# Attention's two z evacuations move from ScalarE to VectorE, and the FFN's last two output groups are emitted as a closure one iteration later

## What is computed

```python
def attn(x):                       # x is layernorm(x)
    q, k, v = x @ Wq.T, x @ Wk.T, x @ Wv.T          # 16 heads x 128
    s = clip(q @ k.T / sqrt(128), -1024, 1024)
    s = s + slope[h] * j + causal(i, j)             # ALiBi bias, causal mask
    return softmax(s) @ v  ->  @ Wo
def ffn(x):                        # x is layernorm(x)
    base = x @ W.T + b
    gates = softmax(top2(x @ gate_w.T + gate_b))    # 8 experts, rank 16
    return base + sum_over_top2(gate * (x @ A_e.T @ B_e.T))
x = x + attn(layernorm(x)); x = x + ffn(layernorm(x))
```

## Time and profile before

| what | us |
|---|---|
| median of the two runs shown | 4926.32 (4838.13 and 5014.51) |
| the profiled execution | 4846.59 |
| its span on the slowest core, 7 | 4845.0 |
| the spans of the eight cores | 4811.6 to 4845.0 |

### The profile page before, as it was taken

One profiled execution on the slowest core, in us unless ns is written; L12 is line 12 of the kernel. 1 busy time (PEld: TensorE's weight loads), 2 busy tenths in 40 slices (PEclk: granted clock), 3 DMA queues, 4 the chain that ended last, 5 costly groups with the idle time before them and its releaser, 6 DMA issues. The chain is left out here.

```text
span 4845.0 us, 65585 instructions; the slowest of 8 cores (4811.6 to 4845.0 us)
## 1 busy us (share of the span) xinstructions
PE 3632.1 (75%) x18452; PEld 1694.7 (35%) x18452; DVE 1615.0 (33%) x4336; ACT 1491.2 (31%) x3694; POOL 110.7 (2%) x210
## 2 busy tenths in 40 slices
PE   3578788898987794676734687888888878937677
PEld 1233344443433341233312343434444433413333
DVE  2222434535353111222312334344453531112223
ACT  5442442525343100212144525334252431001211
POOL 0000000000000001000000000000000000010000
PEclk7668778898988896777867687788889888967778
DMA  3201101011111655111132011110101126451111
GB/s 112 57 14 22 18 14 27 14 23 18 22 20 35 166 157 105 61 61 61 53 109 66 14 23 18 18 23 14 27 14 23 18 45 172 148 105 61 61 61 53
DMA packets 55538, 258.39 MB, mean 53 GB/s; under 512 B 13720, under 2 KB 13984, under 8 KB 34720
## 3 DMA queue, kind: packets, MB, share of 16 engines
q0 software_dynamic: 36464, 119.66, 12.3%
q1 hardware_dynamic: 11824, 84.20, 5.4%
q10 hardware_dynamic: 6912, 50.33, 2.9%
HBM read 273.15 MB, written 67.11 MB: 70 GB/s over the span
## 5 line engine op out<-in xcount | busy, mean ns | idle before, releaser
L812 DVE TENSOR_SCALAR sp<-ps 128x512 f32<-128x512 f32 (+3 forms) x1104 | 634.7, 596 | 227.8 <-ACT prT L876 119.8
L851 ACT ACTIVATE prT<-dg,cstt 128x128 bf16<-128x128 f32 (+1 forms) x576 | 217.6, 388 | 1580.5 <-DVE dg L823 1252.4
L1119 PE MATMUL cb<-wf,cT 128*128 128x512 bf16 x2048 | 536.6, 426 | 83.5 <-DMA wf<-wf 81.8
L876 ACT ACTIVATE prT<-sp,cstt 128x128 bf16<-128x128 f32 (+2 forms) x1368 | 582.3, 494 | 4.6 <-DVE zc L752 1.0
L805 PE MATMUL ps<-QT,KT 128*128 128x512 bf16 (+3 forms) x1104 | 457.2, 481 | 111.5 <-DVE sp L812 67.4
L420 PE MATMUL bp<-wo,zTt 128*128 128x512 bf16 x2048 | 468.1, 392 | 89.7 <-DMA wo<-wo 71.5
L632 PE MATMUL pp<-xnT,wv 128*128 128x512 bf16 x2048 | 485.1, 400 | 0.4
L632 PE MATMUL pp<-xnT,wq 128*128 128x512 bf16 x2048 | 462.0, 387 | 0.0
L632 PE MATMUL pp<-xnT,wk 128*128 128x512 bf16 x2048 | 457.6, 384 | 0.0
L743 PE MATMUL pz<-va,prT 128*128 128x129 bf16 x3652 | 376.3, 258 | 20.7 <-ACT prT L876 9.3
L1119 PEld LDWEIGHTS cb<-wf,cT 128*128 128x128 bf16 x2048 | 216.1, 108 | 389.2 <-issue 210.2
(11 more groups left out here) (105 smaller groups left out, 2463.4 us busy)
## 6 DMA issues: line engine op xcount, KB each, us to landing
bx<-x SPq DMA_DIRECT2D x32, 1024.0 KB, 6.7
x2d<-b POOLq DMA_DIRECT2D x32, 1024.0 KB, 8.8
c<-x2d ACTq DMA_DIRECT2D x32, 1024.0 KB, 4.8
out<-co SPq DMA_DIRECT2D x32, 1024.0 KB, 3.9
prT<-x ACTq DMA_DIRECT2D x16, 1024.0 KB, 4.9
prT<-x SPq DMA_DIRECT2D x16, 1024.0 KB, 5.0
wv<-wv POOLq DMA_DIRECT2D x32, 512.0 KB, 5.3
wq<-wq POOLq DMA_DIRECT2D x32, 512.0 KB, 5.2
```

The source lines that it names most:

```text
L812: lambda e, n=n, bank=bank, buf=buf: e.tensor_scalar(spanb[buf][:, 0:n], psc[bank][:, 0:n], 1024.0, -1024.0, ALU.min, ALU.max),
L851: soff=soff: e.activation(probsT[:, pslot:pslot + min(ncols, 128)], diagb[:, soff:soff + min(ncols, 128)] if ncols == 64 else diagb[:, 0:128],
L876: buf=buf, bcol=bcol: e.activation(probsT[:, pslot: pslot + ncols], spanb[buf][:, soff: soff + ncols], AF.Exp, bias=cst[:, bcol:bcol + 1]),
L1119: lambda e, bi=bi, dc=dc, og=og, bk=bk: e.matmul(b["pb"][bk][:, :], b["xnT2"][bi][:, dc * 128:(dc + 1) * 128], b["wfT"][:, dc * D + og * 5 ...
```

## The change

Two things. In attention, the multiplication of `pz` by the reciprocal and the copy of the transposed block are DVE instructions in place of ACT ones, with the waits changed to match. In the FFN, `finish_og(2)`, `finish_og(3)` and the store become a closure that is called at the top of the next iteration.

```diff
-        first_w.append((s_act, st["pz_guard"][qt % 2]))
+        first_w.append((s_dve, st["pz_guard"][qt % 2]))
...
-        zn = pg.op("scalar",
-                   lambda e, zb=zb, qt=qt: e.activation(
-                       ztm[zb][:, :], pz[qt % 2][:, 0:128], AF.Identity,
-                       scale=zcol[:, 4 + qt % 2:5 + qt % 2]),
-                   inc=s_act,
+        zn = pg.op("vector",
+                   lambda e, zb=zb, qt=qt: e.tensor_scalar(
+                       ztm[zb][:, :], pz[qt % 2][:, 0:128],
+                       zcol[:, 4 + qt % 2:5 + qt % 2], None, ALU.mult),
+                   inc=s_dve,
                    waits=[(s_dve, r), (s_pe, st["ztr_tok_pe"][zb])])
...
-                       waits=[(s_act, zn), st["ptp_copy"]])
+                       waits=[(s_dve, zn), st["ptp_copy"]])
             st["ztr_tok_pe"][zb] = zt
-            st["ptp_copy"] = (s_act, pg.op(
-                "scalar",
-                lambda e, h=h, qt=qt: e.activation(
+            st["ptp_copy"] = (s_dve, pg.op(
+                "vector",
+                lambda e, h=h, qt=qt: e.tensor_copy(
                     zT[:, h * SEQL + qt * 128: h * SEQL + (qt + 1) * 128],
-                    ptp[:, 0:128], AF.Identity),
-                inc=s_act, waits=[(s_pe, zt)]))
+                    ptp[:, 0:128]),
+                inc=s_dve, waits=[(s_pe, zt)]))
...
+    pend_fin = []
     for i in range(NT):
         bi = i % 2
         bi3 = i % 3
+        for _f in pend_fin:
+            _f()
+        pend_fin.clear()
         t_apply = apply_tok[bi3]
...
         base_chunks(2)
         base_chunks(3)
-        finish_og(2, False)
-        mm = finish_og(3, False)
...
+        def fin23(fi=i, fbi=bi, fbi3=bi3, fev4=ev4, ffinish=finish_og):
+            nonlocal wxa_reader
+            ffinish(2, False)
+            mm = ffinish(3, False)
...
+        pend_fin.append(fin23)
+    for _f in pend_fin:
+        _f()
+    pend_fin.clear()
```

More of the change, by code:

```diff
@@ L1155, in _plan_ffn, with finish_og @@
                                (s_pe, wxa_reader)])
-        def finish_og(og, first_delta):
+        def finish_og(og, first_delta, fi=i, fbi=bi, fbi3=bi3, fev4=ev4,
+                      fwxa_tok=wxa_tok):
             bk = og % 2
@@ L1164, in finish_og @@
                       inc=s_pe,
-                      waits=[lora_tok[4]] if (i == 0 and og == 0) else [])
+                      waits=[lora_tok[4]] if (fi == 0 and og == 0) else [])
             m = pg.op("tensor",
@@ L1171, in finish_og @@
                       inc=s_pe,
-                      waits=([(s_dve, wxa_tok)] if first_delta else []) +
-                            ([lora_tok[3]] if (i == 0 and og == 0) else []))
+                      waits=([(s_dve, fwxa_tok)] if first_delta else []) +
+                            ([lora_tok[3]] if (fi == 0 and og == 0) else []))
             ev = pg.op("vector",
-                       lambda e, bi=bi, bi3=bi3, og=og, bk=bk: e.tensor_tensor(
-                           b["outb"][bi][:, og * 512:(og + 1) * 512],
+                       lambda e, fbi=fbi, fbi3=fbi3, og=og, bk=bk:
+                       e.tensor_tensor(
+                           b["outb"][fbi][:, og * 512:(og + 1) * 512],
                            b["pb"][bk][:, :],
-                           b["x2b"][bi3][:, og * 512:(og + 1) * 512], ALU.add),
+                           b["x2b"][fbi3][:, og * 512:(og + 1) * 512],
+                           ALU.add),
                        inc=s_dve,
-                       waits=[(s_pe, m), (sem["dob"][bi], store_tok[bi])])
+                       waits=[(s_pe, m), (sem["dob"][fbi], store_tok[fbi])])
             base_evac[bk] = ev
-            ev4[og] = ev
+            fev4[og] = ev
             return m
@@ L1188, in _plan_ffn @@
         base_chunks(3)
-        finish_og(2, False)
-        mm = finish_og(3, False)
[L1191 to L1198, removed]
+        def fin23(fi=i, fbi=bi, fbi3=bi3, fev4=ev4, ffinish=finish_og):
+            nonlocal wxa_reader
+            ffinish(2, False)
+            mm = ffinish(3, False)
+            wxa_reader = mm
+            xnT2_rd[fbi] = mm
+            ev_out[fbi3] = fev4[-1]
+            store_tok[fbi] = pg.op("sync",
+                                   lambda e, fi=fi, fbi=fbi: e.dma_start(
+                                       out_d.ap()[seq][fi],
+                                       b["outb"][fbi][:, :]),
+                                   inc=sem["dob"][fbi], amt=16,
+                                   waits=[(s_dve, t_) for t_ in fev4])
+        pend_fin.append(fin23)
+    for _f in pend_fin:
+        _f()
+    pend_fin.clear()
 def _host_consts():
```

## The result

The changed kernel takes 1.004 times as long as before, with an interval of 1.0025 to 1.0055: some 19 us slower. Ratios compare fast runs with fast runs; in a slow one the cores of one die show a lower granted clock and take longer. The prediction took 2% as what a measurement of this kernel can tell from no change; the interval is much narrower than that. The forecast had +56 us, with a sum of single terms behind it of +104 and -48. The direction of each term was right, and the small net is what two large terms leave. Both were off, by amounts that add.

The account below looks back on a forecast made before the run. ACT was taken to bound heads 0 to 5, ACT and DVE together the group heads. Over two sequences 104 - 48 = +56 us on 4846.6 gives 4903, stated as 4900; range 4835 to 4965.

Parts of the forecast that it names:

- What bounds the kernel: Attention stretches: ACT is fullest in heads 0 to 5; in group heads ACT (31.91 us) and DVE (29.04) are almost level.
- The price of a block: Per query block, DVE gains 0.19 wait, 0.27 multiplication and 0.14 copy, 0.60 us in all; ACT loses 0.41 us.
- The stretch after: Attention stretches set by DVE's time: heads 0 to 5 give back 24.0 us per sequence, ten group heads cost 52.
- The 9.6: DVE's added time per attention stretch, from 0.60 us for each query block.
- The 2.0: Time per stretch DVE can't fill: 0.6 us before the first clip and the end of the last two accumulations.
- DVE is the fullest engine in every head: All attention stretches: with ACT down by 6.6 us and DVE up by 9.6, DVE is the fullest engine.
- The second way of the prediction: Group heads: ten early blocks cost 6.0 us, six find idle time in the tail; between +5 and +6 us.
- FFN: FFN half of the change: every engine's order and waits stay the same, cost 0.
- The signs: What would show it: DVE busy up 230 us, ACT down 210, group stretches 43 us with DVE at 90% or more.
- A: Group stretches: DVE has room, so not slower; 4799 us, or 4636 if every stretch gains 6.6 us; chance 0.15.
- B: Group stretch tails: PE's clock stays at 1.2 GHz, total 5000 us, 3.2% slower; chance 0.14.
- C: FFN: the change hides the tail of a tile behind the next, below 20 us; chance 0.01.

Follow-up runs that it names:

- the early blocks: Against the kernel before, both instructions on DVE only in the first nine query blocks (qt 0 to 8) of the group heads: profiled execution 4915.9 us.
- the hidden wait: Against the attention half alone, transpose and copy of the block before emitted between reciprocal and multiplication: profiled execution 4799.8 us, group stretches 40.24 us.
- the second copy: Against the attention half alone, DVE copies the transposed block a second time, into a scratch tile, in every block: ratio 1.0104 (1.0026 to 1.0182).
- the late blocks: Against the kernel before, both instructions on DVE only in the last seven query blocks (qt 9 to 15) of the group heads: ratio 0.9978.

## Why the prediction was right or wrong

**What bounds the kernel.** Right. The page's shares of 33% and 31% said nothing; the single stretches did. ACT was the fullest engine in heads 0 to 5 and nearly level with DVE in the group heads, and moving work from one to the other gave -60 and +77 us.

**The price of a block.** Right in each part: 0.35 us for the multiplication (0.351), 0.225 for the copy (0.216), 0.33 from reciprocal to multiplication (0.34). The 0.14 that it took for before, from the reciprocal to the next instruction, was one of several values: the earlier trace rows have 0.23, and the mean in the group stretches, where DVE does not stop for long, is 0.19. The Trainium skill, "Perfetto Trace Analysis", section "Optimizing Scalar/DVE Operations", had made the two 0.04 us dearer; measured from start to start they are 0.27 and 0.13 us (medians), so the multiplication agrees with its overhead of 125 ns on PSUM and the copy is cheaper than by that figure. Its rule, that work can better go to ScalarE where DVE is saturated, holds in the group heads and is what the early blocks showed.

**The stretch after.** This is the step that failed, in the size of its sums and not in the mechanism. The forecast for a group stretch was busy time, sixteen own waits before `dg`, 9.6 us for the blocks and 2.0 us that DVE can't fill: 29.0 + 2.7 + 9.6 + 2.0 = 43.3 us. Head 8 after is 29.0 + 2.8 + 8.7 + 1.2 = 41.7, of a window of 41.8. Over the twenty group stretches the mean rose by 3.8 us where 5.2 was said. Two terms were too large, and one sentence was wrong.

- The 9.6. It counts sixteen blocks, but the stretch ends with the last accumulation, and the last block's reciprocal, multiplication and copy come behind it: the reciprocal starts at 929.44, after the window's end at 929.30. Inside the window DVE has 102 instructions where the earlier trace rows have 72, so 30 more, which is fifteen blocks. They added 6.0 us of busy time (35.1 - 29.0, close to 15 x 0.41) and 2.7 us of own waits, together 8.7. Of the 0.9 us too much, 0.6 is the sixteenth block.
- The 2.0 that DVE "can't fill". In head 8 after, DVE is idle 41.8 - 35.1 = 6.7 us. Of these the 16 own waits before `dg` are 2.8 and the 15 before the multiplication 2.7, so 1.2 are left: 0.64 before the copy of the transposed v, as forecast, and 0.6 for the rest, where the forecast had 1.4.
- "DVE is the fullest engine in every head." In head 1 it is ACT even after the change. By the prediction's own figures the two were level there (35.4 - 6.6 = 28.8 for ACT, 16.6 + 12.3 = 28.9 for DVE), and it did not compare them. The number was right by luck (30.9 forecast, 31.1 measured): neither the hidden wait nor the second copy moved that head by more than 0.2 us. In head 5 no engine sets the stretch alone: the second copy, 2.1 us of DVE work, added 0.7, and the stretch came out at 41.5 where 40.9 was said.

The first two are 1.3 to 1.5 us in each of twenty stretches, 27 us in all. Heads 0, 2, 3 and 4 came out too long by the same sum: 28.9, 33.9, 35.5 and 38.0 were forecast, 27.0, 32.4, 34.1 and 36.4 measured.

Heads 0 to 5 gave 60 us where 48 was said, the group heads cost 77 where 104 was said. 12 + 27 = 39, and +56 - 39 = +17, which is what the stretches show. The net is the small difference of two large terms, so errors of a fifth in one and a third in the other made it three times too large.

The second way of the prediction, by blocks, counted ten blocks without room. The reciprocals say that the loss stops at +4.2 us, some seven blocks' worth, because after the first few blocks part of the new work goes into holes that DVE had in before (its idle time before clips fell from 3.7 to 0.3 us per group stretch); the two kernels with the early and the late blocks confirm where it arises. Its reason, idle time in the tail, was right.

**FFN.** Right: 1.0012 with 1.000 in the interval, the same lists and an FFN stage of the same length.

**The signs.** ACT's busy time fell by 209 us and DVE's rose by 212 where 210 and 230 were named. "DVE at 90% or more" did not follow from the prediction's own sum: (29.0 + 6.6) of 43.3 us is 82%, and 84% was measured; with its own waits DVE is taken for 97% of head 8.

**The rivals.** A (DVE has room) is out for the early blocks and true for the late ones: the point from which it decides was named, the room is in the tail alone. Its 9.6 us of new work would not quite have fitted into the 9 us of idle time in any case. Of B (the clock) one of the two signs came and the cost did not: head 8's tail was granted 0.88 in the window above, below the 0.9 that was named, where it had 0.94, and the projection behind it 1.00. If that clock cost time, the stretches with less of it would be longer. Of the 160 group stretches on the eight cores of the changed kernel, the 66 with a granted clock of at most 0.64 last 41.9 us on average and the 36 with at least 0.68 last 42.0. C (the FFN) came to nothing.

## What to carry to other kernels

Where two engines share a loop, a change that moves work between them has to be priced for each kind of iteration: it gained in twelve stretches and lost in twenty, and the average over both said "nothing". Where the net is the difference of two large terms, count only what lies inside the stretch that is timed (fifteen blocks here, not sixteen), count an engine's waits for its own results as its time, and compare the engines again after adding. And in this kernel a multiplication that reads what DVE has just written waits 0.17 to 0.18 us; the copy of 0.13 us put between the two took 0.105 us per block off the group stretches, so it was nearly free.

## What the runs showed that I had not expected

A stretch can move more than the engine's own instructions would explain. Head 1 lost 8.1 us while ACT lost 16 x 0.41 = 6.6 us of list: its busy time fell from 35.36 to 27.89, 7.5 us, and its idle time from 3.9 to 3.3. The exponentials that stayed are themselves a little shorter there (the 84 of line 876 at 332 ns on average where they had 335, the 32 of line 851 at 333 where they had 341), some 0.5 us. Why was not tested.

The granted clock fell in the group stretches (0.69 to 0.67 over head 8 and 0.64 in the run with the copy twice) without a cost that I could find. That PE waits for DVE there, and a slower matmul ends inside that wait, would explain it, but was not tested. Behind every group stretch of these two kernels the projection was granted 0.99 or 1.00. Behind the emptier stretches of heads 0 and 1, which are at 0.50 to 0.53 in every kernel, it was not: 0.95 in the changed kernel, where these projections take 43.8 and 43.5 us against 41.4 behind head 8, and 0.79 and 0.87 in the profiled execution of before. So a low clock can be carried into the projection and costs time there; the change neither brought that nor took it away. Why it was so much lower in some executions stays open.
